# A gated cross-attention and 4-bit feed-forward layer on one core: other order of the FFN's products, weight split and LayerNorm moments at other places

## The reference, cut to what matters

```python
# x, ctx: (32, 64, 512) float32
x = x + tanh(g_xattn) * xattn(layernorm(x), ctx, ctx, Wq, Wk, Wv, Wo, bo, g)   # linear attention, 8 heads
x = x + tanh(g_ffn) * ffn(layernorm(x), gate, up, down)
# ffn: x2 is (2048, 512); weights are 4 bit, dequantised by groups of 128 along K
gate, up = x2 @ Wg, x2 @ Wu                     # (2048, 1376)
out = (gate * sigmoid(gate) * up) @ Wd          # (2048, 512)
```

## Time and profile before

| | us |
|---|---|
| three runs: median (lowest to highest) | 733.96 (733.6 to 735.58) |
| the profiled execution: its own time | 733.95 |
| its span, first to last instruction | 732.1 |
| PE busy (share of the span) | 681.9 (93%) |
| DVE busy | 585.6 (80%) |
| ACT busy | 475.4 (65%) |
| POOL busy | 350.9 (48%) |

### The profile page before, as it was taken

One profiled execution on the slowest core, in us unless ns is written; L12 is line 12 of the kernel. 1 busy time (PEld: TensorE's weight loads), 2 busy tenths in 40 slices (PEclk: granted clock), 3 DMA queues, 4 the chain that ended last, 5 costly groups with the idle time before them and its releaser, 6 DMA issues.

```text
span 732.1 us, 14401 instructions
## 1 busy us (share of the span) xinstructions
PE 681.9 (93%) x4995; PEld 352.8 (48%) x4995; DVE 585.6 (80%) x774; ACT 475.4 (65%) x841; POOL 350.9 (48%) x455
## 2 busy tenths in 40 slices
PE   5789999999999999999999996999999999999995
PEld 4444554455455545545554542445444444454443
DVE  6567888888888888788888567889988888888885
ACT  4856786677668667767775746567655665665562
POOL 6312212222221322222234663788777867886783
PEclk9999999999999999999999999999999999999998
DMA  4112312330332122112200100000000001000101
GB/s 108 32 37 64 89 46 54 92 90 10 88 89 63 33 77 73 34 49 74 76 6 24 25 6 2 1 0 2 1 29 30 1 0 44 15 1 16 43 1 58
DMA packets 30509, 28.96 MB, mean 40 GB/s; under 512 B 20047, under 2 KB 20186, under 8 KB 30466
## 3 DMA queue, kind: packets, MB, share of 16 engines
q1 hardware_dynamic: 28058, 27.73, 14.0%
q10 hardware_dynamic: 2408, 0.70, 0.4%
HBM read 22.42 MB, written 4.23 MB: 36 GB/s over the span
## 4 chain that ended last, share of the span: by engine, by line
PE 63%; DVE 10%; ACT 8%; issue 7%; POOL 5%; DMA 5%; SPq 1%; DVEq 0%; ACTq 0%; POOLq 0%
PE small L1025 8%; PE small L996 7%; PE pair L982 6%; PE pair L1226 5%; PE pair L1227 4%; DVE acc L1529 4%; PE small L1012 4%; PE pair L1250 4%; DMA rn_rows<-rn_parts 3%; POOL rn_sq L433 3%; PE pair L961 3%; ACT eq L664 3%; PE pair L1262 3%; PE small L1062 3%; PE small L1226 2%
## 5 line engine op out<-in xcount | busy, mean ns | idle before, releaser
L1529 DVE SCALAR_TENSOR_TENSOR acc<-pair,scale_T,acc 128x512 f32<-128x512 f32 (+1 forms) x176 | 131.8, 749 | 27.2 <-ACT acc L782 14.7
L1442 DVE TENSOR_TENSOR eq<-eq,pair 128x1024 f32<-128x1024 f32 x64 | 78.1, 1221 | 54.0 <-PE pair L1079 53.9
L565 POOL TENSOR_TENSOR yT<-yT,y_scaled 128x512 f32<-128x512 f32 (+1 forms) x78 | 100.3, 1287 | 19.6 <-ACT y_scaled L813 18.6
L1226 PE MATMUL pair<-ek,w_gu 128*128 128x512 f16 (+1 forms) x235 | 91.8, 391 | 2.8 <-DVE acc L1529 1.8
L655 ACT ACTIVATE ek<-pair,kneg 128x512 f32<-128x512 f32 x128 | 86.7, 686 | 10.3 <-DVE kneg L1437 10.1
L1227 PE MATMUL pair<-ekT,w_gu 128*128 128x512 f16 (+1 forms) x235 | 89.5, 381 | 0.0
L1434 DVE TENSOR_REDUCE qmax<-pair 128x16 f32<-128x1024 f32 x64 | 77.7, 1214 | 8.1 <-PE pair L961 8.1
L1250 PE MATMUL pair<-in_hi,d_int 128*128 128x512 f32 (+1 forms) x132 | 73.4, 559 | 10.9 <-DVE yT L1572 10.8
L664 ACT ACTIVATE eq<-pair 128x1024 f32<-128x1024 f32 x64 | 65.6, 1025 | 22.6 <-PE pair L1101 22.3
L1437 DVE TENSOR_REDUCE kneg<-pair 128x2 f32<-128x1024 f32 x64 | 77.9, 1218 | 0.6 <-PE pair L982 0.2
L1529 DVE SCALAR_TENSOR_TENSOR acc<-small,scale_T,acc 128x512 f32<-128x512 f32 (+1 forms) x88 | 65.9, 749 | 13.1 <-ACT acc L782 6.5
(11 more groups left out here) (187 smaller groups left out, 1434.4 us busy)
## 6 DMA issues: line engine op xcount, KB each, us to landing
xall<-in_x SPq DMA_DIRECT2D x16, 256.0 KB, 2.6
ctx_raw<-in_ctx SPq DMA_DIRECT2D x16, 256.0 KB, 2.8
out_x<-xall SPq DMA_DIRECT2D x16, 256.0 KB, 2.0
zero<-zeros_plus SPq DMA_DIRECT2D x8, 344.0 KB, 5.5
packed<-in_L_ffn_gate_qweight SPq DMA_DIRECT2D x4, 688.0 KB
packed<-in_L_ffn_up_qweight SPq DMA_DIRECT2D x4, 688.0 KB
packed<-in_L_ffn_down_qweight SPq DMA_DIRECT2D x10, 256.0 KB
zero<-zeros_plus SPq DMA_DIRECT2D x5, 256.0 KB, 5.0
```

The source lines that it names most:

```text
L565: pool.tensor_tensor(yT16[:, nt, :] if it == IT - 1 else total, total, y_scaled[:, nt, :], ALU.add).then_inc(z_add, 1)
L1226: pe.matmul(gu_bank[count % 3][0:w, :], lhsT, xT_hi[:, g, rows], start=True, stop=False)
L1442: dve.tensor_tensor(e, e, dve_pair[:, :, :], ALU.mult).then_inc(q_norm, 1)
L1529: dve.scalar_tensor_tensor(out=acc[0:w, n % 2, m, :], in0=gu_bank[(8 * n + job) % 3][0:w, :], scalar=scale_T[0:w, it, 4 * m + g:4 * m + g ...
```

## The change

It makes these edits.

1. PE's high products come in the order nt 0, 1, 3, 2 (HIGH_ORDER). Behind the last unit the products of unit 42 run high and low for 0, 1, 3 and then for 2; ACT's `scaled(42, 0)` stands ahead of its `high_part(43)`, DVE's `last_low_part` ahead of `add_sum(42, 2)`, which waits for all of unit 42's products.
2. `rows_transposed` moves from job 3 to job 1, `fed_forward` from behind the last add to between the adds 3 and 5.
3. `plain_scaled` runs earlier on POOL, `plain_high` in ACT's drain, `plain_low` on POOL instead of DVE; `wd` gets another address through a padding tensor. A Silu of 8 columns stands at the end of ACT's drain. ACT's `outputs` of the last pair moves ahead of `silu(0)`, `ffn_normalised(8)` and `(9)` behind `silu(1)` and `silu(2)`.
4. POOL's inverse norm of the last pair stands behind `activated(1)`. The moments of pairs 14 and 15 are `bn_aggr` and three small operations on DVE (`late_moments`, `late_factors`) and one power on POOL (`late_deviation`).
5. In the first step: Wk comes by SP's queue and Wq by ACT's; DVE's memsets stand ahead of the first statistics; the first moments are `bn_aggr` and an addition on DVE and a power on POOL; POOL's `ctx_low(0)` waits for `xn`; the low part of Wq and the transposes of Wo and `fold_weights` come later.

The diff, cut to its core:

```diff
+HIGH_ORDER = (0, 1, 3, 2)
...
+        sb("between", [P, 1536])
         wd = sb("wd", [P, IT, P])
...
-            load_weight_twice(sp, wq, wq_sb, wq_in)
+            load_weight_twice(sp, wk, wk_sb, wk_in)
...
-            layernorm(0)
+            pool.wait_ge(first_moments, 2)
+            pool.tensor_tensor(ln_work[:, 7:8], ln_work[:, 6:7], minus_half[:, 0:1], ALU.pow).then_inc(rstd_ready, 1)
+            pool.wait_ge(xn_ready, 1)
             ctx_low(0, 0)
...
+            def late_deviation(k):
+                pool.wait_ge(ln2_late, 4 * (k - PAIRS + 2) + 2)
+                pool.tensor_tensor(ln2_work[:, k, 7:8], ln2_work[:, k, 3:4], minus_half[:, 0:1], ALU.pow).then_inc(ln2_late, 1)
...
             def plain_scaled():
-                pool.wait_ge(f_mm, PAIRS)
+                pool.wait_ge(f_mm, PAIRS - 1)
+                pool.wait_ge(q_mm, 4 * PAIRS)
                 pool.wait_ge(w_int, PAIRS - 2)
                 pool.wait_ge(d_scale_in, 16)
...
             ffn_normalised(5)
+            plain_scaled()
             ffn_normalised(6)
             step(PAIRS, 0, True, False)
             ffn_normalised(7)
-            plain_scaled()
+            plain_low()
             for n in range(UNITS):
                 if n:
                     activated(n - 1)
+                if n == 2:
+                    step(PAIRS + 1, 1, True, False)
                 add_sum(n - 3, 1)
                 if n:
                     low_part(n - 1)
-                if n == 1:
-                    step(PAIRS + 1, 1, True, False)
-                if n == 2:
-                    second_moments(2)
+                if n == 3:
+                    late_deviation(PAIRS - 2)
                 if n == 5:
-                    second_moments(3)
+                    late_deviation(PAIRS - 1)
                 add_sum(n - 2, 0)
...
                     transposed(3)
+                    plain_high()
                     transposed(4)
+                    act.activation(act_gate[:, 0:8], ones[:, :], ACT.Silu)
                     return
...
                 if n == 0:
                     transposed(7)
+                    step(PAIRS + 1, PAIRS // 2, 1, False, False, True, drain=True)
                 silu(n)
-                if n == 0:
+                if n == 1:
+                    ffn_normalised(8)
+                if n == 2:
+                    ffn_normalised(9)
                     act.activation(ident16[:, :], ident[:, :], ACT.Copy).then_inc(ident16_made, 1)
-                    step(PAIRS + 1, PAIRS // 2, 1, False, False, True, drain=True)
-                    plain_high()
-                    ffn_normalised(8)
-                    ffn_normalised(9)
...
+            scaled(UNITS - 2, 0)
             high_part(UNITS - 1)
-            scaled(UNITS - 2, 0)
...
                     if n >= 2 and job < NJ:
-                        high_product(n - 2, job)
+                        high_product(n - 2, HIGH_ORDER[job])
...
-                    if j and job == 3 and 3 <= it < 3 + TPC:
+                    if j and job == 1 and 3 <= it < 3 + TPC:
                         rows_transposed(j - 1, it - 3)
-            for nt in range(NJ):
-                high_product(UNITS - 2, nt)
-            for nt in range(NJ):
-                low_product(UNITS - 2, nt)
-            for nt in range(NJ):
+            for product in (high_product, low_product):
+                for nt in (0, 1, 3):
+                    product(UNITS - 2, nt)
+            high_product(UNITS - 2, 2)
+            low_product(UNITS - 2, 2)
+            for nt in HIGH_ORDER:
                 high_product(UNITS - 1, nt)
...
+            def late_moments(k):
+                dve.wait_ge(bn2_done, k + 1)
+                dve.bn_aggr(ln2_work[:, k, 0:2], stats2[:, k, :]).then_inc(ln2_late, 1)
+                dve.wait_ge(ln2_late, 4 * (k - PAIRS + 2) + 1)
+                dve.tensor_scalar(ln2_work[:, k, 3:4], ln2_work[:, k, 1:2], EPS, None, ALU.add).then_inc(ln2_late, 1)
...
-                dve.wait_ge(z_mm, NJ * n + nt + 1)
+                dve.wait_ge(z_mm, NJ * n + (NJ if n == UNITS - 2 else nt + 1))
...
                 if it == 0 and job == 7:
                     attended(PAIRS - 2)
+                    late_moments(PAIRS - 2)
+                if it == 4 and job == 3:
+                    late_factors(PAIRS - 2)
                 if it == 3 and job == 7:
                     attended(PAIRS - 1)
+                if it == 4 and job == 7:
+                    late_moments(PAIRS - 1)
+                if it == 6 and job == 3:
+                    late_factors(PAIRS - 1)
...
-                if it == 1 and job == 4:
-                    plain_low()
...
-                if j and 3 <= it < 3 + TPC:
-                    fed_forward(j - 1, it - 3)
+                    if j and job == GH and 3 <= it < 3 + TPC:
+                        fed_forward(j - 1, it - 3)
             last_activated()
             add_sum(UNITS - 3, 2)
+            last_low_part()
             add_sum(UNITS - 2, 2)
-            last_low_part()
```

More of the change, by code:

```diff
@@ L533, in plain_scaled, with plain_low @@
                                        d_scale[0:rows, its, :], ALU.mult).then_inc(d_scaled, 1)
+            def plain_low():
+                for part, its in enumerate((slice(0, IT - 1), slice(IT - 1, IT))):
+                    rows = P if its.start == 0 else width(IT - 1)
+                    pool.wait_ge(d_hi, part + 1)
+                    pool.tensor_tensor(wd_lo[0:rows, its, :], wd[0:rows, its, :], wd_hi[0:rows, its, :].bitcast(F32),
+                                       ALU.subtract).then_inc(d_lo, 1)
             def activated(n):
@@ L760, in transposed, with plain_high @@
                                ACT.Copy).then_inc(xT_hi_ready, 1)
+            def plain_high():
+                for part, its in enumerate((slice(0, IT - 1), slice(IT - 1, IT))):
+                    rows = P if its.start == 0 else width(IT - 1)
+                    act.wait_ge(d_scaled, part + 1)
+                    act.activation(wd_hi[0:rows, its, :], wd[0:rows, its, :], ACT.Copy).then_inc(d_hi, 1)
             step(0, 0, 0, True, False, False)
@@ L797, in high_part @@
                 act.activation(in_hi[0:w, n % 2, :], inter[0:w, n % 2, :], ACT.Copy).then_inc(in_hi_ready, 1)
-            def plain_high():
-                for part, its in enumerate((slice(0, IT - 1), slice(IT - 1, IT))):
-                    rows = P if its.start == 0 else width(IT - 1)
-                    act.wait_ge(d_scaled, part + 1)
-                    act.activation(wd_hi[0:rows, its, :], wd[0:rows, its, :], ACT.Copy).then_inc(d_hi, 1)
             def scaled(n, nt):
@@ L823, in ffn_normalised @@
             def ffn_normalised(k):
-                part = [n for n, (start, _) in enumerate(ln2_parts) if k >= start][-1]
-                act.wait_ge(ln2_step, 11 * (part + 1))
+                if k < PAIRS - 2:
+                    act.wait_ge(ln2_step, 22)
+                else:
+                    act.wait_ge(ln2_late, 4 * (k - PAIRS + 2) + 4)
                 act.wait_ge(xT_mm, k - 3)
@@ L875, in _, with output_weights @@
             last.then_inc(weights_T, 1)
-            pe.wait_ge(wvo_in, 48)
-            for t in range(OT):
-                last = pe.transpose(wo_ps[:, t * C:(t + 1) * C], wo_sb[:, t * P:(t + 1) * P], ident[0:C, 0:C])
-            last.then_inc(weights_T, 1)
+            def output_weights():
+                pe.wait_ge(wvo_in, 48)
+                for t in range(OT):
+                    last = pe.transpose(wo_ps[:, t * C:(t + 1) * C], wo_sb[:, t * P:(t + 1) * P], ident[0:C, 0:C])
+                last.then_inc(weights_T, 1)
             def fold_weights():
@@ L976, in k_logits @@
                             pe.wait_ge(kt_evac, 4 * p)
+                        else:
+                            pe.wait_ge(wT_lo_ready, 2)
                     else:
@@ L1169, in step @@
                 k_logits(1)
+                if not combine:
+                    fold_weights()
                 output(0)
@@ L1341, in _, with query_weights_low @@
             dve.memset(ss_sq[:, :], 0.0).then_inc(dve_consts, 1)
-            layernorm_apply(0)
-            for n, (ps, hi, lo, sign) in enumerate(((wq_ps, wqT_hi, wqT_lo, 1.0), (wk_ps, wkT_hi, wkT_lo, -1.0))):
-                dve.wait_ge(wT_hi_ready, n + 1)
-                dve.scalar_tensor_tensor(out=lo[:, :], in0=ps, scalar=sign, in1=hi[:, :].bitcast(F32), op0=ALU.mult,
-                                         op1=ALU.subtract).then_inc(wT_lo_ready, 1)
+            layernorm_stats(0, 0, 0)
+            dve.wait_ge(ln_stats, 1)
+            dve.bn_aggr(ln_work[:, 0:2], stats[:, :]).then_inc(first_moments, 1)
+            dve.wait_ge(first_moments, 1)
+            dve.tensor_scalar(ln_work[:, 6:7], ln_work[:, 1:2], EPS, None, ALU.add).then_inc(first_moments, 1)
+            layernorm_apply(0)
+            dve.wait_ge(wT_hi_ready, 2)
```

(14 more changed lines are left out.)

26 lines of the change are left out of this document (15 added, 11 removed).

## The result

The changed kernel takes 714.39 us, median of 4 runs (712.53 to 715.82); the kernel before, beside it on the same chip, 734.64 (4 runs, 733.6 to 735.58). The ratio is 0.9724, 95% interval 0.9705 to 0.9744. The profiled execution took 714.0, span 712.2, against 733.95 and 732.1. The forecast was 714.6, range 710.5 to 721.5.

What follows compares the result with a forecast made beforehand. A loop through DVE's addition, PE's product and ACT, no single engine, was taken to set 5.85 us per plain unit. Gains 3.2 + 7.9 + 3.7 + 0.4 + 1.6 + 2.2 + 0.3 = 19.3 took 733.95 to 714.6, range 710.5 to 721.5.

Steps and rivals of the forecast that it cites:

- Order and fed_forward: Units 13 to end: new order gains 3.2 us on 18 plain intervals, moving fed_forward 7.9 on 12 transposing ones.
- Banks take over: Rival: three banks for eight jobs make PE wait for DVE's adds in every unit; 720.6 us, chance 0.18.
- Beginning: Start of the feed-forward: shorter DVE path and reordered POOL work, net 3.7 us, plus 0.4 in unit 4; stage bounds 2 to 5.5.
- on DVE's path the waits of 1.42, 2.01 and 0.62 and `plain_low` go: Beginning of the feed-forward: three DVE waits and plain_low's 1.6 us to the next add vanish, 5.65 us.
- The late moments: Beginning of the feed-forward: two small dependent DVE operations, 0.3 us each with hand-over, cost 0.6 together.
- The 1.1 that I had put down as a bound: Beginning of the feed-forward: some 1.1 us more if POOL's products keep out a small DVE moments operation.
- The 0.4 for the softened wait in unit 4: Unit 4: the new order softens PE's first wait on DVE, gaining 0.4 us more.
- Second moments of pair 15: Interval 481.47 to 488.74: POOL's eleven small operations hold up activated; removing them gains 1.6 us.
- Tail: Last units: seven matmuls of unit 42 run in PE's wait for DVE; gain 2.2 us, bounds 1 and 2.5.
- Start: First step: first logits 1 to 2 us earlier, but only 0.3 us gained; bounds -0.5 and 1.3.
- the walk of the queues at one matmul spacing: First step: queues walked to 0.4 us at the third maxima and 0.2 at tile 3's exponentials; 0.3 taken.
- the clock stays low: Rival in the first feed-forward units: at 1.2 GHz each unit loses 5.67 us; four give 737.3, chance 0.02.

Runs made afterwards that it cites:

- rows_spread: Changed kernel with each chunk's row transposes and fed_forward in its units 3, 5, 7, 9 instead of 3 to 6: 712.73 us, ratio 0.97.
- table_late: Changed kernel without the Silu of 8 columns ending ACT's drain, so the table loads before the first silu again: 712.81 us, ratio 0.9692.
- order_old: Changed kernel with the loop's four high products back in order 0, 1, 2, 3; tail and fed_forward stay as changed: 717.16 us, ratio 0.9758.
- attended_late: Changed kernel with DVE's residual, statistics and first moments of pair 14 moved from unit 0, job 7, to unit 2, job 4: 713.63 us, ratio 0.9707.
- residual_split: Changed kernel with pair 14's residual behind bound_norms at unit 1, job 7, its statistics and first moments at unit 2, job 4: 712.81 us, ratio 0.9695.
- rows_late: Changed kernel with fed_forward back behind its unit's last add and row transposes back at job 3; new product order stays: 714.99 us, ratio 0.9717.
- start_old: Changed kernel with the whole first step as before: load queues, weight fold, first moments on POOL, Wq's low part: 715.69 us, ratio 0.9731.
- tail_old: Changed kernel with the old order of the last units on PE, DVE and ACT: 715.4 us, ratio 0.9748.

## Why the prediction was right, point by point

- **Order and fed_forward.** Predicted 3.2 + 7.9 = 11.1 behind unit 13, measured 11.26, with plain intervals at 5.67. Transposing ones were taken at 6.07 and are 5.89 to 6.06, one of them (unit 27) 6.29; one or two plain ones behind each group are longer as well, 5.89 to 6.06, so that a transposing unit costs about 6.1 in all. The sum was right; its division into an order's 3.2 and a move's 7.9 holds only if the move is counted first. Counted first, the order brings 10.26.
- **Banks take over.** In plain units the rival fell: they take PE's 5.67. In the transposing units it came in a small form. A matmul for gate and up starts when an add of DVE ends (545.68 and the pair of adds to 547.28, then 547.34), 0.57 behind the product instead of 0.42:

```profile
545.68 1.60 DVE L1579 SCALAR_TENSOR_TENSOR acc<-pair,scale_T,acc 128x512 f32<-128x512 f32 x2
```

```profile
546.77 0.58 PE L1277 MATMUL pair<-in_hi,d_int 128*128 128x512 f32 x1
547.34 0.39 PE L1253 MATMUL pair<-ek,w_gu 128*128 128x512 f16 x1
```

  The view of waits shows 0.4 us of this in all, since the product lasts until 547.35 by its modelled end. By starts, 13-43 is 175.32 against 18 x 5.67 + 12 x 5.91 = 173.0 of PE's own work, so 2.3 us are left there; rows_spread wins 1.04 of them.
- **Beginning.** Predicted 4.1 by unit 4, measured 2.88 + 1.20 = 4.08. The size was right and its working in part by luck. The step "on DVE's path the waits of 1.42, 2.01 and 0.62 and `plain_low` go" counted the 1.42 whole and laid it to the table load with what stands behind it; the add at 445.95 came to 445.08 only, since DVE's own work fills the time, and by table_late moving the load brought nothing. `plain_low` is 1.24 on DVE and 1.32 by the stretches instead of 1.6. The late moments cost 0.42, not 0.6. The 1.1 that I had put down as a bound, POOL holding a DVE operation, did not come at the moments; the residual was held, 1.68 against 0.74, but it had taken 1.46 before, which I had not listed. The 0.4 for the softened wait in unit 4 is 0.24 (7.24 in order_old, 7.00 in the changed kernel). That leaves some 1.6 of the 4.08 for the new places of `plain_high`, ACT's `outputs` and `ffn_normalised`, and POOL's inverse norm. None of them was undone alone, so that part is inferred and not shown.
- **Second moments of pair 15.** Predicted 1.6, measured 1.27 by undoing both pairs; the two traces show 1.99 from unit 4 to 13, the order's 0.5 there among it (order_old is 0.04 + 0.46 longer).
- **Tail.** Predicted 2.2, measured 2.29 between the traces and 2.39 undone alone.
- **Start.** Predicted 0.3; 0 in the profiled pair. The step that failed is the walk of the queues at one matmul spacing. PE's spacing there is 0.23 or 0.42, and which holds when differs from run to run.
- **The clock.** The rival "the clock stays low" had a chance of 0.02. It did not decide: one low stretch (0.50) lies there in either kernel, 446.29 to 449.70 before and 445.42 to 448.84 in the changed one. But the clock does act in this stage: it cost attended_late 1.53 of the 3.60 by which its unit 3 grew.
- **The range.** Its lower end, 710.5, is 1.2 below what its own terms give (714.6 - 1.9 - 1 = 711.7). The time lies far from it, so nothing hung on that.

## What to carry to other kernels

Look for the loop that runs through an unconditional order of issue: when a wait ends exactly as another engine's operation ends, unit after unit, try to put independent work of the waiting engine ahead of the waiting instruction. Here that alone, with `fed_forward` in its old place, shortened thirty units by 10.26 us; shortening either side was not tried. When two edits lengthen the slack of one loop, undo each alone and both together, since their gains are not a sum. And before moving two-input vector work, look at what POOL starts beside it in its new place, and how long PE would stand.

## What was unexpected of the hardware

PE's clock fell in the feed-forward around waits of 2 to 2.5 us. In the changed kernel PE waits 2.51 us and then runs so:

```profile
445.88 0.61 PE L1253 MATMUL pair<-ek,w_gu 128*128 128x512 f16 x1 [2.51 <-DVE acc L1579]
446.29 0.63 PE L1254 MATMUL pair<-ekT,w_gu 128*128 128x512 f16 x1
...
448.42 0.59 PE L1253 MATMUL pair<-ek,w_gu 128*128 128x512 f16 x1
448.85 0.38 PE L1254 MATMUL pair<-ekT,w_gu 128*128 128x512 f16 x1
```

Its windows, with PE's busy time and the granted clock (the fourth column) around it:

```profile
443.00:445.88 2.88, 0.38 (x2) 0.92 0.02 1
445.88:448.85 2.97, 2.96 (x8) 0.50 0.00 0
448.85:454.00 5.15, 5.15 (x26) 1.00 0.01 2
```

0.50 is the level of 1.2 GHz, 1.00 that of 2.4 GHz. In attended_late a wait of 1.96 was followed, after 0.85 more at the full rate, by a stretch with 0.53 granted (456.10 to 459.74), although PE had been busy for 9.05 of the 11.95 us ahead of it. In residual_split PE had shorter waits and the clock stayed at 1.00.

In the changed kernel this low stretch cost nothing: from job 4 of unit 1 to the first high product PE takes 3.88 (445.88 to 449.76), and residual_split, at full clock, takes 3.88 too (443.61 to 447.49), where PE waits 0.25 at a time for DVE's adds and 0.42 for ACT. In these runs it costs more the later it comes. Five profiled runs have the same code from "first" to the mark in unit 2, and PE's starts in them agree to 0.02 us up to 14.4 behind "first". Then they part:

| kernel | the clock falls, us behind "first" | first-2 |
|---|---|---|
| changed | 11.44 | 20.77 |
| rows_late | 11.73 | 20.91 |
| start_old | 11.98 | 21.01 |
| tail_old | 12.48 | 21.24 |
| rows_spread | 13.30 | 21.67 |

That is the 0.9 of spread in "first-2". What makes attended_late's two groups of runs, 3.6 us apart, was not traced; the low stretch is worth 1.53 in the traced run.

At the start the column of the granted clock misleads. The products for the exponentials of the first tile, in the changed kernel (0.42 apart) and in rows_spread (0.23 apart):

```profile
22.03 0.66 PE L1122 MATMUL pair<-xs_hi,wqT_lo 64*128 64x512 f32 x2
22.45 0.66 PE L1122 MATMUL pair<-xs_lo,wqT_hi 64*128 64x512 f32 x2
```

```profile
20.52 0.43 PE L1122 MATMUL pair<-xs_hi,wqT_lo 64*128 64x512 f32 x2
20.75 0.42 PE L1122 MATMUL pair<-xs_lo,wqT_hi 64*128 64x512 f32 x2
```

```profile
20.00:22.00 2.00, 1.11 (x5) 1.00 0.01 4
22.00:24.00 2.00, 2.00 (x22) 1.00 0.09 22
```

(the last two are windows of the changed kernel). The column reads 1.00 although the starts lie 0.42 apart, but the trace of this run holds no clock record before 25.58, and the column shows 1.00 where there is none. The first record is of 1.00, and there the spacing falls to 0.22 (from 25.80 on). In the kernel before the first record begins at 19.62 and the wide spacing ends at 19.5; in rows_spread a record of 1.00 covers 12.89 to 40.20, with the narrow spacing; in tail_old one of 0.50 covers 20.02 to 23.44, and the starts at 20.70, 21.12 and 21.55 are wide apart. So wherever there is a record the two agree, and the spacing of starts tells the clock where there is none.

The place of these stretches is what moves "first". In the changed kernel another low stretch lies at 42.65 to 46.06, in tail_old none between 23.44 and 443; against the changed kernel, PE in tail_old is 1.7 us ahead at 31 us, 3.1 at 52 us and 3.2 at "first".
